# Layer 1 of a graph network on Trainium2: forward sums from gathered rows instead of a dense matrix product

## The reference, cut to what matters

```python
def _weighted_mean_agg(ft, w, src, dst, n_nodes):
    m = ft[src] * w[:, None]
    msum = jax.ops.segment_sum(m, dst, num_segments=n_nodes)
    wsum = jax.ops.segment_sum(w, dst, num_segments=n_nodes)
    safe = jnp.where(wsum > 0, wsum, 1.0)
    return jnp.where((wsum > 0)[:, None], msum / safe[:, None], 0.0)
neigh1 = _weighted_mean_agg(feat, w, src, dst, n)   # "forward": sums at dst
neigh2 = _weighted_mean_agg(feat, w, dst, src, n)   # "backward": sums at src
hn = jnp.concatenate([neigh1 @ W1.T, neigh2 @ W2.T], axis=1)
gi = hn @ w_ih.T + b_ih
gh = feat @ w_hh.T + b_hh
...
return nn_ + z * (feat - nn_)
```

## Time and profile before

| | |
|---|---|
| three runs | 10148.71, 10153.24, 10154.86 us; median 10153.24 us |
| the profiled execution | 10154.51 us, its span 10152.8 us |
| TensorE busy in the span | 9102.2 us (90%), mean granted clock 0.962 |
| VectorE / ScalarE / GpSimd busy | 5836.0 / 4659.0 / 3272.2 us |
| TensorE busy from 250 to 3450 us, in the sums stage | 3075.71 of 3200 us, granted clock 0.98 |
| VectorE / ScalarE / GpSimd busy there | 2105.35 / 1127.65 / 66.00 us |

### The profile page before, as it was taken

The page is one execution under the profiler, slowest core; times in us unless marked ns, Lnnn a source line. Parts: engine busy times, 40 slices in busy tenths (PEclk is TensorE's granted clock), DMA queues, the critical chain, the costliest instruction groups (busy, mean ns, idle before and its releaser), DMA issues. The chain is left out here.

```text
span 10152.8 us, 237386 instructions
## 1 busy us (share of the span) xinstructions
PE 9102.2 (90%) x62443; PEld 7436.0 (73%) x62444; DVE 5836.0 (57%) x12039; ACT 4659.0 (46%) x11625; POOL 3272.2 (32%) x3463
## 2 busy tenths in 40 slices
PE   6999999999999869999897788888887599999998
PEld 5999999999999747777565566666665476666666
DVE  7666666666666457776212455555554455555555
ACT  3333333333333244444101476776775455555555
POOL 2000000000000000000000477777774377777775
PEclk7999999999999889999898899999999799999999
DMA  2000000000000002222453444444442122222222
GB/s 78 3 3 3 3 3 3 3 3 3 3 3 3 11 37 110 114 114 101 167 193 118 142 118 118 118 118 118 118 118 89 50 73 73 73 73 72 72 73 69
DMA packets 372611, 702.00 MB, mean 69 GB/s; under 512 B 102415, under 2 KB 268371, under 8 KB 352468
## 3 DMA queue, kind: packets, MB, share of 16 engines
q0 software_dynamic: 136128, 335.76, 11.8%
q1 hardware_dynamic: 236052, 359.58, 10.1%
HBM read 546.68 MB, written 148.25 MB: 68 GB/s over the span
## 5 line engine op out<-in xcount | busy, mean ns | idle before, releaser
L1603 POOL DMA_INDIRECT x<-table,p_gidx x1632 | 1542.3, 945 | 2458.7 <-ACT p_gidx L1640 1990.6
L2104 POOL DMA_INDIRECT c_G<-table,c_gidx x1632 | 1555.7, 953 | 505.4 <-issue 493.1
L687 PE MATMUL g_ps_cell<-g_kw,g_loh 128*128 128x98 f32 x9472 | 1240.6, 275 | 93.0 <-DVE g_kw L617 47.3
L662 ACT COPY g_AT<-g_ps_turn 128x384 f32<-128x384 f32 (+1 forms) x1258 | 578.8, 466 | 1580.5 <-PE g_ps_turn L717 1580.5
L687 PEld LDWEIGHTS g_ps_cell<-g_kw,g_loh 128*128 128x128 f32 x9472 | 1168.0, 194 | 102.1 <-issue 71.9
L697 PE MATMUL g_ps_slot<-h,g_A 128*128 128x129 f32 x7252 | 1056.8, 282 | 56.2 <-issue 56.2
L579 POOL DMA_INDIRECT g_hrow<-table,dst_tab x74 | 69.8, 943 | 3192.4 <-PE g_ps_rev L708 3191.9
L1694 PE MATMUL p_ps_sum<-x 128*96 128x256 f32 x3264 | 893.0, 397 | 177.1 <-DVE hid L1629 164.7
L602 DVE TENSOR_TENSOR x<-x,g_ps_rev 128x387 f32<-128x387 f32 (+1 forms) x1258 | 670.8, 538 | 649.0 <-PE g_ps_rev L708 649.0
L708 PE MATMUL g_ps_rev<-g_hrow,g_AT 128*128 128x129 f32 x7252 | 1032.7, 281 | 0.5 <-ACT g_AT L662 0.5
L697 PEld LDWEIGHTS g_ps_slot<-h,g_A 128*128 128x128 f32 x7252 | 923.1, 194 | 59.0 <-issue 59.0
(11 more groups left out here) (343 smaller groups left out, 15544.7 us busy)
## 6 DMA issues: line engine op xcount, KB each, us to landing
adj_save<-a_A SPq DMA_DIRECT2D x74, 1568.0 KB, 5.1
a_A<-adj_save SPq DMA_DIRECT2D x74, 1568.0 KB, 6.6
c_ed<-in_edge_dram SPq DMA_DIRECT2D x1632, 25.0 KB
x<-table,p_gidx POOLq DMA_INDIRECT x1632
p_lhs<-in_edge_dram SPq DMA_DIRECT2D x1632, 16.0 KB
c_G<-table,c_gidx POOLq DMA_INDIRECT x1632
table<-m_rows SPq DMA_DIRECT2D x17, 384.0 KB, 2.5
x<-in_x_dram SPq DMA_DIRECT2D x1, 3328.0 KB, 11.0
```

Source lines behind the costliest of these rows:

```text
L662: s.copy(AT[:, b, 0:w], ps_turn[b][:, 0:w]).then_inc(at_ready, 1)
L687: last = pe.matmul(ps_cell[q % 2][:, r * KEYS:(r + 1) * KEYS], loh[:, b, cell, :], kw[:, b, cell, :], start=True, stop=True)
L1603: g.indirect_dma_start(G[:, H * b + q, :], None, table2, bass.IndirectOffsetOnAxis(ap=gidx[:, b, q:q + 1], axis=0)).then_inc(gathered[b], 16)
L2104: g.indirect_dma_start(G[:, H * b + q, :], None, table, bass.IndirectOffsetOnAxis(ap=gidx[:, b, q:q + 1], axis=0)).then_inc(gathered[b], 16)
```

## The change

The forward sums no longer use `A`. Edges are sorted by target, so the 1563 tiles are taken as 391 runs of four consecutive tiles. Each batch n gets six runs e = 0 to 5 (one for each bucket that a run touches, 444 in all). A run gathers for each of its four tiles the 128 source rows from `table` by an indirect DMA of GpSimd (`g_G`, three buffers), ScalarE scales them by the edge weights (`g_Gw`), VectorE makes a one-hot of the target for each tile in one comparison (`g_roh`), TensorE multiplies and sums the four (`g_ps_run`), and VectorE adds the result to one bucket of `fwd`. Where these stand in the 16 steps is set by four tables. `forward`, the placing, `g_sums`, `g_poh` and the counting are gone. `h` no longer stays in SBUF: the nodes stage loads it back from `table` (`u_hin`), and computes its means two chunks ahead instead of one. The lists stage makes the runs' lists, with four more gathers of 128 x 1536 words, and saves them to DRAM (`run_save`).

```diff
+RQ = 4
+GR = 3
+OH_AT = {0: 0, 3: 1, 5: 2, 8: 3, 11: 4, 13: 5}
+SCALE_AT = {1: 0, 4: 1, 6: 2, 9: 3, 12: 4, 14: 5}
+RUN_AT = {2: 0, 5: 1, 7: 2, 10: 3, 13: 4, 15: 5}
+ADD_AT = {3: (0, 0), 6: (0, 1), 8: (0, 2), 11: (0, 3), 14: (0, 4), 0: (-1, 5)}
...
                     def _(g):
-                        for m in range(NBATCH):
-                            if m >= 2:
-                                g.wait_ge(rev_made, TGS * (m - 1))
-                            g.indirect_dma_start(hrow[:, m % 2, 0:D], None, table,
-                                                 bass.IndirectOffsetOnAxis(ap=dst_tab[:, m % 2, m // 2:m // 2 + 1], axis=0)).then_inc(gathered[m % 2], 16)
+                        for n in range(NBATCH):
+                            if n >= 2:
+                                g.wait_ge(rev_made, TGS * (n - 1))
+                            g.indirect_dma_start(hrow[:, n % 2, 0:D], None, table,
+                                                 bass.IndirectOffsetOnAxis(ap=dst_tab[:, n % 2, n // 2:n // 2 + 1], axis=0)).then_inc(gathered[n % 2], 16)
+                            g.wait_ge(runs_in[n % 2], 16 * (n // 2 + 1))
+                            for e in range(RPB):
+                                m = RPB * n + e
+                                if m >= GR:
+                                    g.wait_ge(weighted, m - GR + 1)
+                                for q in range(RQ):
+                                    g.indirect_dma_start(G[:, e % GR, q, 0:D], None, table,
+                                                         bass.IndirectOffsetOnAxis(ap=runs[:, n % 2, 0, RQ * e + q:RQ * e + q + 1], axis=0)
+                                                         ).then_inc(rows_in[e % GR], 16)
...
+                        def add_run(n, s):
...
+                            at = bass.ds(run_bucket(v, n + back, e), 1)
+                            v.wait_ge(run_made, m + 1)
+                            v.wait_ge(added, m + 1)
+                            v.tensor_tensor(fwd[:, at, :], fwd[:, at, :], ps_run[e % 2][:, 0:D + 2].rearrange("p (o d) -> p o d", o=1),
+                                            ALU.add).then_inc(added, 1)
+                        def make_run_oh(n, s, iteration, bb):
...
+                            for q in range(RQ):
+                                last = v.tensor_scalar(roh[:, e % 2, q, :], iota, runs[:, bb, 1, RQ * e + q:RQ * e + q + 1].bitcast(F32), None, ALU.is_equal)
+                            last.then_inc(roh_made, 1)
...
+                        def weigh_run(n, bb, e):
+
+                            if not (isinstance(n, int) and n == 0 and e < 2):
+                                s.wait_ge(run_made, RPB * n + e - 1)
+                            s.wait_ge(rows_in[e % GR], 16 * RQ * (RPB // GR * n + e // GR + 1))
+                            for q in range(RQ):
+                                last = s.activation(Gw[:, e % 2, q, 0:D + 1], G[:, e % GR, q, :], ACT.Identity,
+                                                    scale=runs[:, bb, 2, RQ * e + q:RQ * e + q + 1].bitcast(F32))
+                            last.then_inc(weighted, 1)
...
-                        def forward(m, b, q):
...
+                        def sum_run(n, e):
+
+                            m = RPB * n + e
+                            pe.wait_ge(roh_made, m + 1)
+                            pe.wait_ge(weighted, m + 1)
+                            if not (isinstance(m, int) and m < 2):
+                                pe.wait_ge(added, m)
+                            for q in range(RQ):
+                                last = pe.matmul(ps_run[e % 2][:, 0:D + 2], roh[:, e % 2, q, :], Gw[:, e % 2, q, :], start=q == 0, stop=q == RQ - 1)
+                            last.then_inc(run_made, 1)
...
                         for c in range(NCH):
                             if c >= 2:
+                                sp.wait_ge(turned, c - 1)
+                            sp.dma_start(hin[:, c % 2, 0:count(c), :], tiles(table)[:, tiles_in(c), :]).then_inc(h_in[c % 2], 16)
+                            if c >= 2:
                                 sp.wait_ge(added, c - 1)
                             sp.dma_start(xin[:, c % 2, 0:count(c), :], a["x"][:, tiles_in(c), :]).then_inc(x_in[c % 2], 16)
...
                         def turn(c):
                             pe.wait_ge(means_ready, 2 * c + 2)
+                            pe.wait_ge(h_in[c % 2], 16 * (c // 2 + 1))
```

More of the change, by code:

```diff
@@ L149, in build @@
         bucket_row = sb("bucket_row", [1, PG * P // H], I32)
+        run_row = sb("run_row", [1, RG * P // 2], I32)
         deg = sb("deg", [P, NT, 2])
@@ L310, in _ @@
-                        then(v.tensor_copy(first[:, :, :], whole[:, :, :]))
-                        v.wait_ge(consts, 9)
-                        then(v.tensor_tensor(first[:, :, :], first[:, :, :], tno[:, :].unsqueeze(1).to_broadcast([P, 2, TK]), ALU.add))
-                        then(v.memset(first[0:1, :, 0:1], 0.0))
-                        then(v.tensor_copy(whole[:, :, :], first[:, :, :]))
-                        v.tensor_scalar(part_i[:, 0, :, :], whole[:, :, :], 7, None, ALU.arith_shift_right)
@@ new lines, in _ @@
+                        then(v.tensor_scalar(whole[:, TK:2 * TK], whole[:, TK:2 * TK], 683.0, None, ALU.mult))
+                        then(v.tensor_scalar(whole[:, TK:2 * TK], whole[:, TK:2 * TK], 11, None, ALU.arith_shift_right))
+                        then(v.tensor_copy(first[:, :], whole[:, :]))
+                        v.wait_ge(consts, 10)
+                        then(v.tensor_tensor(first[:, :], first[:, :], tno[:, :], ALU.add))
+                        for at in columns:
+                            last = v.memset(first[0:1, at.start:at.start + 1], 0.0)
@@ L390, in _ @@
                             then(v.tensor_scalar(here[:, 1, 0:m, :], rel[:, 0:m, :], 1.0, None, ALU.is_equal))
-                            for j in range(GRP):
-                                last = v.tensor_reduce(cnt_c[:, j, g0:g0 + m], here[:, j, 0:m, :], AX_X, ALU.add)
-                            then(last)
                             then(v.tensor_tensor(here[:, 0, 0:m, :], here[:, 0, 0:m, :], here[:, 1, 0:m, :], ALU.add))
@@ L461, in _ @@
                                 s.copy(w_tab[:, cols], pt[at % 4][:, 2 * P:3 * P]).then_inc(taken, 1)
-                            if which == 0 and g0 + m == LG:
-                                s.wait_ge(cnts_turned, 1)
-                                for j in range(GRP):
-                                    last = s.copy(cnts[:, :, j, :], ps_cnts[0:LG, j * P:(j + 1) * P].rearrange("g (h c) -> g h c", h=2))
-                                last.then_inc(cnts_made, 1)
-                        s.wait_ge(small_turned, 2)
-                        s.copy(cnt_tab[:, :, :].rearrange("p k g -> p (k g)"), ps_small[:, 4 * LG:6 * LG])
         def buckets_of(eng, n):
@@ L541, in stage_gru_sums @@
                 hrow = sb("g_hrow", [P, 2, D + 1], F32, ctx)
-                sums = sb("g_sums", [P, 2, D + 2], F32, ctx)
-                poh = sb("g_poh", [P, 2, GRP * P], F32, ctx)
+                runs = sb("g_runs", [P, 2, 3, RD], I32, ctx)
+                G = sb("g_G", [P, GR, RQ, D + 1], F32, ctx)
+                Gw = sb("g_Gw", [P, 2, RQ, D + 2], F32, ctx)
+                roh = sb("g_roh", [P, 2, RQ, P], F32, ctx)
                 rev = rev_in_x()
@@ L571, in stage_gru_sums, with _, load @@
                 with nc.Block() as block:
+                    @block.sync
+                    def _(sp):
+                        def load(i, bb):
+                            n = 2 * i + bb
+                            if not (isinstance(n, int) and n < 2):
+                                sp.wait_ge(weighted, RPB * (n - 1))
+                                sp.wait_ge(roh_made, RPB * (n - 1))
+                            sp.dma_start(runs[:, bb, :, :], run_save[:, :, bass.ds(n * RD, RD)]).then_inc(runs_in[bb], 16)
+                        over_batches(sp, load)
                     @block.gpsimd
```

266 lines of the change are left out of this document (149 added, 117 removed).

## The result

The changed kernel takes 10347.02 us (median of 4 runs, 10345.79 to 10351.61), the kernel before 10154.05 beside it: a ratio of 1.0186, 95% interval 1.0168 to 1.0204. It is slower by 193 us, twice the +95 that I forecast. That is inside the range given, and just above the 10,175 to 10,340 of the forecast's own. The profiled execution has a span of 10349.9 us against 10152.8, so +197.1 to be explained.

What follows compares the result with a forecast made beforehand. TensorE was taken to bound the sums stage. Sums +83, first batches +3, nodes +13 and lists -4 gave +95 on 10154.5, so 10,250 us; range 10,080 to 10,420, the forecast's own 10,175 to 10,340.

Steps and rivals of the forecast that it cites:

- What bounds the kernel: Sums stage: TensorE sets the time, busy 3075.71 of 3200 us; a batch takes 42.0 us.
- What the change gives TensorE: Sums stage: 11.9 us of passes removed, 5.6 added; TensorE's work in a batch goes from 42.0 to 35.7 us.
- The place of the wait: Once a batch, at its first row gathers, behind GpSimd's wait for backward products: TensorE idle 5.2 us, bounds 4.4 to 6.2.
- Gathers follow each other every 1.25 us: GpSimd's queue: a batch's fourth row gather starts 4 x 1.25 us behind the target rows' gather.
- The clock: TensorE behind the wait for gathers: 3.2 us at half clock, so 1.6 us lost in a batch, bounds 0 and 3.2.
- VectorE's lateness: Late in a batch VectorE falls about 1.0 us behind; TensorE then waits 0.8 us, bounds 0 and 1.7.
- ScalarE: Scalings for the five later groups of a batch: they hardly wait, 0.2 us for all, bounds 0 and 1.8.
- The loop's turns: Sums stage: the existing slow stretch lies partly beside the gathers' wait, giving back some 0.7 us in every second batch.
- The sum: A sums-stage batch: 43.5 against 42.0 us, +1.5; +83 over 72 batches after the turns' 25, +3 for the first two.
- Nodes: Nodes stage: u_hin arrives late, about 3.9 us after the add; +1.9 for ten chunks, less 6, so +13.
- Lists: Lists stage: VectorE's counts go, four large gathers and a longer save are added; -4, bounds -10 and +10.
- the clearly slower one: Sums stage: VectorE becomes the bound outside the wait, 37.6 us in a batch; about 10,510 in all, chance 0.12.

Runs made afterwards that it cites:

- e5: Changed kernel with three edits: target rows gathered later in their batch, numbers for g_loh read from PSUM, h loaded a chunk earlier; 9580.17 us, ratio 0.9426.
- e6: Changed kernel with GpSimd gathering a batch's target rows behind the row gathers of its third group of four tiles, not ahead of the first; 9808.64 us, ratio 0.9663.
- run 0: No follow-up kernel: the first (e = 0) of a batch's six groups of four tiles in the changed kernel; TensorE waits 6.9 us there in the mean.
- e7: Changed kernel with the numbers that g_loh's comparison reads copied to PSUM, and all forward sums in one bank; 10246.82 us, ratio 1.0088.
- e8: Changed kernel with 28 products that nothing reads on TensorE ahead of each batch's first wait for gathered rows; 10380.79 us, ratio 1.0219.
- e10: Changed kernel with g_loh's numbers in PSUM, one bank for forward sums, and 22 unread products ahead of each batch's first wait for rows; 10319.81 us, ratio 1.016.
- e9: Changed kernel with SyncE loading h for chunk c+1 ahead of its wait for the add of chunk c-2; 10242.16 us, ratio 1.009.

## Why the prediction was half right

**What bounds the kernel: right. What the change gives TensorE: right in kind, short by 1.3 us.** Step by step the new work is a little dearer than forecast. A plain step takes 1.89 us (I had 1.86), and a run with the slightly longer turning ahead of it adds 1.04 (0.94): 16 x 1.89 + 6 x 1.04 + 0.5 for the last products = 37.0 us, not 35.7. The records of all batches give 37.1, and 37.2 in e5 and e6.

**The place of the wait: right,** and shown by e6: once a batch, at run 0, behind GpSimd's wait. **Its size was the step that failed**: "Gathers follow each other every 1.25 us". I had that from the earlier trace rows, which show gathers under one-operand comparisons and under nothing; in this stage the gathers also start under `g_loh` and `g_kw`. The four row gathers take 6.89 us instead of 5.0, and the wait is 6.9 instead of 5.2, outside my bound of 6.2. It was shown by e7. I asked of the comparisons that the change adds whether they hold GpSimd, and not of the VectorE work that was there already.

**The clock: mechanism right, size 2.4 us for a batch in the mean (1.5 to 3.2), not 1.6.** But 1.0 of these the kernel before lost already, at its turns. So the change adds 1.4, and I had 1.6 less 0.35. In the earlier trace rows TensorE idles 5.92 us; here 6.87. In the batch shown run 0 and step 3 take 1.87 + 3.01 us in place of 0.98 + 1.89. What I had not seen, and e8 showed, is that this loss was partly free: without it GpSimd is late for the later runs.

**VectorE's lateness: right for every second batch.** Around a loop's turn TensorE waits twice, 1.1 us together, of which 0.52 at k = 16 (I had 0.8 in every batch); in the batches inside the body it doesn't wait. **ScalarE: right,** the other five runs hardly wait.

**The loop's turns: a term that I put at almost nothing.** Averages over batches 8 to 71, as GpSimd's gathers of target rows come: before 42.7 us within the body and 47.1 across the turn (I worked with 42.0 from one batch, at the low end); now 46.4 and 47.5. A turn cost 4.4 us more and costs 1.2. In the kernel before TensorE idles 3.5 us at a turn, in two pieces, of which the earlier trace rows show only the second:

```profile
1621.07 1.13 PE L687 MATMUL g_ps_cell<-g_kw,g_loh 128*128 128x98 f32 x8 [1.77 <-issue]
1622.04 0.30 PE L697 MATMUL g_ps_slot<-h,g_A 128*128 128x129 f32 x1
1624.27 1.23 PE L697 MATMUL g_ps_slot<-h,g_A 128*128 128x129 f32 x5 [1.93 <-issue]
```

In the changed kernel both are gone, 1.8 us a batch that my sum kept. The long wait doesn't hide them: in e5 TensorE waits for almost nothing (0.46 us a batch), and there is no such gap either. The changed queue has 323 matmul passes in a batch where the kernel before has 377 and e10, which has the gap again, 367. But e8 has 379 and no gap, and idles 3.5 us a batch ahead of runs. Which of this decides was not tried.

**The sum.** Work 1.3 and the wait 1.5 too cheap (rows and ScalarE together), the clock 0.2, the first batches 13 us in all; against it the turn's 1.8 and VectorE's 0.25 that I had too much. So my +1.15 a batch against +2.05 is a near miss in which large errors partly cancelled. That the total fell inside the range owes something to luck.

**Nodes: right in mechanism,** `u_hin` is late: TensorE turns 3.7 us behind the issue of x's load that the add releases (I had 3.9 behind the add); 19.5 against 19.0 us a chunk, +16.0 against +13.

**Lists: wrong sign.** I took VectorE's counts as what the stage ends on. It ends on the last save, and ahead of that ScalarE copies the run table's 16 tiles, in two copies each, 0.69 us a tile, from 99.46 to 111.07. The save that was the last one before comes 5.3 us earlier (99.08 against 104.35), about what I had hoped for; the run table then adds 12.0, and 1.4 more pass from the save to the next stage. That is +8.1 where I had -4: of a moved step I counted the gathers and the save but not the engine that fills the table.

Of the rivals, the clearly slower one did not come by its own mechanism: VectorE is busy 34.5 of a batch's 46.95 us.

## What to carry to other kernels

An in-order queue that mixes two kinds of transfers makes each wait for the other's condition: look at what stands ahead of a new load before asking how long it takes. Here the two orders (GpSimd's, SyncE's) cost 538 and 105 us, and turning both around, with the numbers in PSUM, made the change worth 5.7%. Take the price of an instruction from rows beside the same neighbours, not only from rows of the same shape. And a loss found in one engine is only worth its size if no other engine is just behind; e8 fills an idle stretch, wins back the clock, and is slower.

## What was not expected of the hardware

- A gather from GpSimd takes 0.94 to 0.95 us, but 1.93 in the mean and up to 3.0 when it starts under `g_loh`, a VectorE instruction with two inputs in SBUF. Of these 390 gathers 233 end 0.78 to 0.86 us behind the end of `g_loh` (one of 1.55 us from 1642.09, under `g_loh` from 1641.61 to 1642.83), and 128 as long behind the end of the next instruction, `g_kw` (2.4 to 3.0 us; the second gather of run 0 is such a one). The other 29 start within 0.1 us around `g_loh`'s start and take at most 1.0 us. What decides whether a gather is held through the second instruction was not settled.
- Reading the numbers from PSUM costs VectorE nothing: `g_loh` takes 1214 ns so, and 1217 from SBUF.
- In the nodes stage the period fell from 19.5 to 9.5 us when a wait of 7.7 us was taken away; the other 2.3 are half of the time that TensorE works at a granted clock of 0.50 in a chunk (a turning of 8 passes takes 1.94 us there, and 1.04 in e9).
